# Rows for a token sort: transposed by DMA from the fp16 halves instead of by fp32 transposes on TensorE

## The reference

```python
xp = x @ Wx + b
h_t = tanh(xp_t + h_{t-1} @ Wh)               # 1024 steps, 2 sequences
shared = silu(h @ shared_w1.T) @ shared_w2.T   # 256 -> 1024 -> 256
logits = h @ gate_w.T                          # 8 experts
gates, idx = top_k(logits, 2); gates = softmax(gates)
selected = sum over the two chosen e of gate_e * (silu(h @ experts_w1[e].T) @ experts_w2[e].T)
out = x + shared + selected
```

## Time and profile before

| | us |
|---|---|
| median of 3 runs | 385.0 (383.47 to 388.58) |
| the profiled execution, its own time | 381.38 |
| its span in the trace | 379.7 |
| PE busy | 356.2 (94%) |
| DVE busy | 200.2 (53%) |
| ACT busy | 244.1 (64%) |
| POOL busy | 108.5 (29%) |
| granted TensorE clock, mean | 0.991 of full speed |

### The profile page before, as it was taken

The page is one execution under the profiler, slowest core; times in us unless marked ns, Lnnn a source line. Parts: engine busy times, 40 slices in busy tenths (PEclk is TensorE's granted clock), DMA queues, the critical chain, the costliest instruction groups (busy, mean ns, idle before and its releaser), DMA issues.

```text
span 379.7 us, 8904 instructions
## 1 busy us (share of the span) xinstructions
PE 356.2 (94%) x2458; PEld 253.0 (67%) x2459; DVE 200.2 (53%) x415; ACT 244.1 (64%) x478; POOL 108.5 (29%) x99
## 2 busy tenths in 40 slices
PE   5989999997997998999999999999999999999981
PEld 4758889964664675666667666667766666666660
DVE  0089999979996988964333323333323333232310
ACT  3777788888556778865555665556665556665530
POOL 1100010000276788600123333223333133332241
PEclk9999999999999999999999999999999999999996
DMA  6999999607697979999898998889988989989992
GB/s 194 422 421 434 428 407 334 194 4 124 87 199 182 225 180 226 235 194 196 176 129 153 168 155 155 147 149 156 158 149 154 148 142 158 148 159 147 152 127 28
DMA packets 158173, 73.50 MB, mean 194 GB/s; under 512 B 140736, under 2 KB 155200, under 8 KB 156992
## 3 DMA queue, kind: packets, MB, share of 16 engines
q1 hardware_dynamic: 146672, 59.83, 66.9%
q0 software_dynamic: 6864, 9.11, 16.9%
q10 hardware_dynamic: 4608, 4.20, 4.1%
HBM read 23.68 MB, written 16.53 MB: 106 GB/s over the span
## 4 chain that ended last, share of the span: by engine, by line
PE 80%; ACT 6%; DMA 5%; issue 3%; DVE 2%; another core or an unknown queue 1%; ACTq 1%; POOL 0%; SPq 0%; DVEq 0%; POOLq 0%
PE py L1138 32%; PE z L1033 30%; PE z L1047 8%; PE z L982 3%; PE z L1014 3%; DMA space<-recurrence_w 2%; DMA space<-space 2%; ACT space L799 1%; ACT space L876 1%; PE px L1025 1%; PE py L982 1%; PE z L995 1%; DMA space<-x_cols 1%; ACTq L896 1%
## 5 line engine op out<-in xcount | busy, mean ns | idle before, releaser
L1138 PE MATMUL py<-w_slots,space 128*128 (+1 forms) x1272 | 148.4, 273 | 7.4 <-DMA space<-recurrence_w 3.7
L1033 PE MATMUL z<-w_slots,x 128*128 (+1 forms) x636 | 145.9, 379 | 0.8 <-issue 0.8
L1138 PEld LDWEIGHTS py<-w_slots,space 128*128 128x128 f16 x1272 | 123.8, 98 | 33.1 <-issue 3.5
L1033 PEld LDWEIGHTS z<-w_slots,x 128*128 128x128 f16 x636 | 62.1, 98 | 65.0 <-issue 1.2
L453 POOL DMA_INDIRECT out<-space x37 | 57.5, 1553 | 157.0 <-issue 65.2
L876 ACT ACTIVATE space<-z,tile_scales 128x512 f32<-128x512 f32 x106 | 71.8, 678 | 41.3 <-PE z L1033 34.1
L582 DVE SCALAR_TENSOR_TENSOR recurrence_w<-space,tile_scales,recurrence_w 128x512 f16<-128x512 f32 x54 | 40.5, 750 | 71.7 <-ACT recurrence_w L881 65.6
L582 DVE SCALAR_TENSOR_TENSOR space<-space,tile_scales 128x512 f16<-128x512 f32 x52 | 39.0, 750 | 57.7 <-ACT space L881 42.4
L528 DVE SCALAR_TENSOR_TENSOR w_slots<-w_slots,w_scale 128x1024 f16<-128x1024 f32 x36 | 46.2, 1283 | 1.3 <-issue 0.3
L881 ACT ACTIVATE recurrence_w<-space,tile_scales 128x512 f16<-128x512 f32 x54 | 39.0, 722 | 8.7 <-ACT space L876 2.5
L430 POOL DMA_INDIRECT sorted_rows<-space x32 | 39.1, 1221 | 17.5 <-issue 13.1
(11 more groups left out here) (114 smaller groups left out, 178.9 us busy)
## 6 DMA issues: line engine op xcount, KB each, us to landing
w_slots<-weights SPq DMA_DIRECT2D x9, 2048.0 KB, 30.5
sorted_rows<-pad_row SPq DMA_DIRECT2D x1, 5070.0 KB, 60.2
space<-x_rows ACTq DMA_DIRECT2D x16, 128.0 KB
out<-space ACTq DMA_DIRECT2D x16, 128.0 KB
space<-x_cols SPq DMA_DIRECT2D x1, 1024.0 KB, 8.6
space<-recurrence_w SPq DMA_TRANSPOSE x54
space<-space SPq DMA_TRANSPOSE x52
x<-sorted_rows SPq DMA_TRANSPOSE x39
```

What stands on the lines that cost most here:

```text
L1033: last = nc.tensor.matmul(Z[u % 2][h][:], x16[:, u, x_part, k], weight(f, k * HID + h * BANK, BANK, part), start=k == 0 and x_part == 0 an ...
L1138: last = nc.tensor.matmul(PY[p][:, 0:D], hiddenT[:, p, low, q], weight(f, MATRIX + q * D, D, part), start=q == 0 and not low and part == 0 ...
```

## The change

The three functions that turned the rows on PE, ACT and DVE (`rows`, `sort_row`, `row_low`) are gone, and with them the PSUM bank PX1 and three semaphores. SP gets `turn_row`: one transposing DMA for each tile, from `x16[:, t % RING]` (128 x 512 fp16) into the row of `hr`. `ROWS_AT` says behind which `turn(g)` it is issued: tiles 0, 1 and 2 behind `turn(0)`, tile 3 behind `turn(1)`, none behind `turn(2)`, 4 and 5 behind `turn(3)`, 6 and 7 behind `turn(4)`, and tile g + 3 behind `turn(g)` from g = 5 on. It waits for `x_lo_ok`, for `routed` at tile 4 (and so for all behind it), and for `sorted_ok` from tile 8 on.

The states' halves are made three tiles ahead (`STATES_AT`): tiles 2 and 3 at g = 0, tile g + 3 at g. Before ACT writes tile t >= 4 to the ring of four, it waits for `row_in[t % RING]`, the landing of the row DMA of tile t - 4. POOL's scatters wait for `row_in` in place of `row_ok`. A row of `hr` is 4 fp32 numbers longer (`ROW_PITCH`).

```diff
@@ -52,6 +52,7 @@
...
 ROW = D + META
+ROW_PITCH = ROW + 4
 SORT_RING = 8
...
@@ -87,8 +88,8 @@
...
 AHEAD = 2
-SORT_FROM = 2
-SORT_TILES = TILES // 2
+ROWS_AT = {0: (0, 1, 2), 1: (3,), 3: (4, 5), 4: (6, 7), **{t - 3: (t,) for t in range(8, TILES)}}
+STATES_AT = {0: (2, 3), **{t - 3: (t,) for t in range(4, TILES)}}
 EARLY_WIDES = 6 * WIDES - 2
...
@@ -171,10 +172,10 @@
...
 
-        hr = carve(SORT_RING, ROW)
+        hr = carve(SORT_RING, ROW_PITCH)
         hr16 = hr.rearrange("p u r -> p (u r)").bitcast(F16).rearrange("p (u r) -> p u r", u=SORT_RING)
         after_rows = at[0]
-        at[0] = RING * ROW
+        at[0] = RING * ROW_PITCH
         onehot = carve(TOP, TILES, E)
...
@@ -229,8 +230,7 @@
...
         ahead = [Z[0], Z[1], PY]
-        PX, PX1 = (ctx.enter_context(nc.psum_tensor(f"px{u}", [P, BANK], F32)) for u in range(2))
-        row_bank = [PX, PX1]
+        PX = ctx.enter_context(nc.psum_tensor("px", [P, BANK], F32))
 
...
@@ -264,7 +264,8 @@
...
         turned = [[sem(f"turned_{part}{p}") for p in range(2)] for part in ("hi", "lo")]
-        row_mm, row_hi, row_ok, row_copied = sem("row_mm"), sem("row_hi"), sem("row_ok"), sem("row_copied")
+        row_in = [sem(f"row_in{u}") for u in range(RING)]
+        row_copied = sem("row_copied")
         sorted_ok = [sem(f"sorted_ok{u}") for u in range(SORT_RING)]
...
@@ -343,8 +344,20 @@
...
 
+            def turn_row(t):
+
+                sp.wait_ge(x_lo_ok, t + 1)
+                if t == RING:
+                    sp.wait_ge(routed, 1)
+                if t >= SORT_RING:
+                    sp.wait_ge(sorted_ok[t % SORT_RING], 16 * TOP)
+                sp.dma_start_transpose(hr16[:, t % SORT_RING, 0:2 * D].rearrange("p (a n) -> p a n", n=P),
+                                       x16[:, t % RING].rearrange("p a k n -> p (a k n)")).then_inc(row_in[t % RING], 16)
+
             for g in range(TILES):
                 turn(g, g % 2)
+                for t in ROWS_AT.get(g, ()):
+                    turn_row(t)
                 if g == TILES - 3:
...
@@ -425,11 +438,11 @@
...
                     pool.wait_ge(row_copied, t - SORT_RING + 1)
-                waited(row_ok, t + 1)
+                waited(row_in[t % RING], 16 * (t // RING + 1))
                 for k in range(TOP):
...
                         out=sorted_slots, out_offset=bass.IndirectOffsetOnAxis(slots_u[:, t, k:k + 1], 0),
-                        in_=hr[:, t % SORT_RING], in_offset=None).then_inc(sorted_ok[t % SORT_RING], 16)
+                        in_=hr[:, t % SORT_RING, 0:ROW], in_offset=None).then_inc(sorted_ok[t % SORT_RING], 16)
                 if RING <= t < TILES - RING:
...
@@ -584,11 +597,6 @@
...
 
-            def row_low(t):
-                dve.wait_ge(row_hi, t + 1)
-                nc.vector.scalar_tensor_tensor(hr16[:, t % SORT_RING, D:2 * D], row_bank[t % 2][:, 0:D], STATE_SCALE,
-                                               hr16[:, t % SORT_RING, 0:D], ALU.mult, ALU.subtract).then_inc(row_ok, 1)
-
             def shared_y(g):
...
@@ -710,7 +718,8 @@
...
             route_gap()
-            states_low(2)
+            for t in STATES_AT[0]:
+                states_low(t)
             for h in range(HALVES):
...
@@ -718,15 +727,9 @@
...
                 hidden_low(g, g % 2, n, 0)
-                row = 2 * (g - 1 - SORT_FROM)
-                sorting = 0 <= row < TILES
-                if g + AHEAD < TILES:
-                    states_low(g + AHEAD)
-                if sorting:
-                    row_low(row)
+                for t in STATES_AT.get(g, ()):
+                    states_low(t)
                 hidden_low(g, g % 2, n, 1)
-                if sorting:
-                    row_low(row + 1)
                 if g == 1:
...
@@ -880,14 +883,6 @@
...
 
-            def sort_row(t):
-                act.wait_ge(row_mm, t + 1)
-                if t == RING:
-                    act.wait_ge(routed, 1)
-                if t >= SORT_RING:
-                    act.wait_ge(sorted_ok[t % SORT_RING], 16 * TOP)
-                nc.scalar.mul(hr16[:, t % SORT_RING, 0:D], row_bank[t % 2][:, 0:D], STATE_SCALE).then_inc(row_hi, 1)
-
             def store(g):
...
@@ -907,26 +902,22 @@
...
             hidden_half(0, 0, None, 0)
-            shared_rows(2, x_hi_ok)
+            for t in STATES_AT[0]:
+                shared_rows(t, x_hi_ok)
             hidden_half(0, 0, None, 1)
...
             for g in range(1, TILES):
-                row = 2 * (g - 1 - SORT_FROM)
-                sorting = 0 <= row < TILES
                 n = 16 * (g // 2) if g >= 2 else None
                 hidden_half(g, g % 2, n, 0)
-                if g + AHEAD < TILES:
-                    shared_rows(g + AHEAD, x_hi_ok)
-                elif g + 1 == TILES:
+                for t in STATES_AT.get(g, ()):
+                    act.wait_ge(row_in[t % RING], 16 * (t // RING))
+                    shared_rows(t, x_hi_ok)
+                if g + 1 == TILES:
                     act.wait_ge(tiles_ok, 1)
-                if sorting:
-                    sort_row(row)
                 hidden_half(g, g % 2, n, 1)
-                if sorting:
-                    sort_row(row + 1)
                 if g <= WIDES // 2:
...
@@ -1140,23 +1131,10 @@
...
 
-            def rows(t):
-
-                if t >= 2:
-                    pe.wait_ge(row_ok, t - 1)
-                for k in range(K):
-                    last = nc.tensor.transpose(row_bank[t % 2][:, k * P:(k + 1) * P], states[:, k, t + 1], identity[:])
-                last.then_inc(row_mm, 1)
-
             def expert(t):
...
             for g in range(TILES):
-                sorting = SORT_FROM <= g < SORT_FROM + SORT_TILES
-                if g == SORT_FROM:
-                    pe.wait_ge(prefix_read, 1)
-                if sorting:
-                    rows(2 * (g - SORT_FROM))
                 if g + AHEAD == TILES:
...
@@ -1164,8 +1142,6 @@
...
                     up(g + AHEAD, (g + AHEAD) % RING, expert(g + AHEAD - TILES), 16)
-                if sorting:
-                    rows(2 * (g - SORT_FROM) + 1)
                 down(g, g % 2, 16 * (g // 2 + 1), SHARED)
...
             def iteration(t, u, n, arrived, up_next=True):

```

## The result

The changed kernel takes 390.7 us (median of 4 runs, 388.1 to 391.8), the kernel before beside it 384.5 (383.5 to 388.6). The ratio is 1.0174 [1.0136, 1.0213]: slower by 1.7%, where 381.5 was forecast, and outside the range of 375.5 to 389.5. The profiled execution of after took 391.55 us with a span of 389.8, against 381.38 and 379.7. So there are 10.1 us to be found between two traces.

What follows compares the result with a forecast made beforehand. PE was taken to bound the kernel, with DVE until about 122 us and the DMA engines from 105 us near their limit. -1.5 - 1.8 - 1.2 + 0.5 + 0.5 = -3.5 us gave 381.5 us (median), range 375.5 to 389.5.

Steps and rivals of the forecast that it cites:

- The start: At g = 1 ACT waits for row 0 and goes on 4.6 us late; `hidden_low(1, 1)` on DVE starts 2.7 us late.
- To `down(5)`: From `hidden_low(1, 1)` to `down(5)`: DVE loses six `row_low` and some idle time, so `down(5)` comes 1.5 us earlier.
- both idle times: DVE's waits of 1.69 and 0.99 us for ACT before `shared_y(3)`, both after ACT's hold of 4.96 us.
- Edits with no cost: Edits priced at nothing: the pitch of the rows, one PSUM bank less, the fewer waits of POOL.
- The upper bound: Worst case for `down(5)`: +1.0 us if ACT's hold comes back elsewhere and the row lands late.
- Rows and late halves: PE from `down(5)` to `down(10)`: -1.8 us for eight rows' transposes gone, -1.2 (0 to -2.4) for turned halves less late.
- DMA engines: Tiles g = 10 to 13: the rows' added packets fill the DMA engines and cost +0.5 us (0 to +6).
- the rival: DMA engines as the bound: at a share of 1.12 a tile takes 5.9 us; 382.4 profiled, 386 median; chance 0.21.
- the slower rival: On SP's ring, tiles 3 to 13, a row costs as much as a whole half: +7.0, 388.4 or 392; chance 0.12.
- the DMAs in series: Each transposing DMA keeps the next one out, so sixteen rows cost 30 us: 411 us; chance 0.01.
- The hand-over: SP waits at g = 13 for all scatters, row 15 coming late, before the first load: +0.5 us (0 to +2).
- The forecast's list: Signs of being wrong: turned halves of 7 us or more, later `row_in` waits, PE standing over 2 us at `down(14)` or `up(16)`.

Runs made afterwards that it cites:

- f1_paced: The changed kernel, with POOL waiting for `up(t + 2)` before the scatters of tiles 4 to 8; 380.7 us, 0.9975 of the kernel before.
- f4_one_pause: The changed kernel, with POOL waiting for `up(6)` before the scatters of tile 4 alone; 381.1 us, 0.9966 of the kernel before.
- f2: The kernel before, with POOL's first scatter waiting until row 5 is ready; 396.6 us, 1.0354 of the kernel before.
- g2: The kernel before, with POOL's scatter of row 2 waiting for the first half of `up(6)`; 387.3 us, 1.0082 of the kernel before.
- g3_pause_early: The changed kernel with rows 0 and 1 issued ahead of `turn(0)` and one POOL pause at tile 4; 379.1 us, 0.9898 of the kernel before.
- g1: As g3_pause_early, and from g = 5 on the row's DMA goes between the two halves of `turn(g)`; 378.0 us, 0.9869 of the kernel before.
- e4: The kernel before with the states' halves made three tiles ahead, rows still turned on PE; 382.3 us, 1.0021 of the kernel before.
- f3: As g1, but with the POOL waits of f1_paced (tiles 4 to 8); 381.7 us, 0.997 of the kernel before.

## Why the prediction was wrong

**The start: right.** Row 0 held ACT for 4.09 us (4.6 forecast), and it went on at 93.45 (93.4 forecast), by the timeline of ACT of the changed kernel:

```profile
93.45 0.42 ACT L828 ACTIVATE x<-states 128x256 f16<-128x256 f32 x1 [4.09 <-DMA space<-x]
```

`hidden_low(1, 1)` started at 95.32, 95.1 forecast. The row itself took about 2.5 us from its issue at 90.9, in the bounds of 1.24 and 3.75 and below the 3.0 taken.

**To `down(5)`: the step that failed.** "After: 95.1 + 29.7 - 2.5 = 122.3 with both idle times, 119.6 with neither", and from this 120.6 was taken and `down(5)` counted at -1.5 us. DVE's part of it held: `shared_y(3)` started at 119.66, close to the end with neither idle time. PE had begun `up(7)` at 117.88 and would have been through at 120.5, so `down(5)` 2.1 us earlier than before, not later. What came was 133.41; without the stand, f1_paced has `down(5)` at 121.29 and f4_one_pause at 121.99. The step took the lists of ACT, DVE and SP for all that PE can wait for, and had POOL down as relieved: under "Edits with no cost" stand "the fewer waits of POOL". These waits were the pauses in POOL's run. With `row_ok` gone, which ACT and DVE had fed at their own pace, 18 scatters follow closely on one another, and after seven to twelve of a run PE starts its matmuls one at a time (nine in the changed kernel). This cost 12.9 us (120.5 to 133.41) and 1.3 for the lower clock behind it. Not all of it comes back with a pause: the trace of f4_one_pause is 11.4 us shorter than the changed kernel's, and the two ratios are 8 us apart. f1, f4 and f2 show cause and remedy: one pause of 1.94 us removes it, and a run made long and close in the kernel before brings it.

**The upper bound missed too.** "+1.0 if the hold comes back elsewhere" allowed for the 4.96 us hold of the earlier trace rows to come again at its old size. It was a row of the trace that no semaphore explained, and I gave it a small price and no mechanism. It is probably of the same kind: ACT stood at 111.28, 8 us into a run of eight scatters, and PE had a gap of 0.72 us ("issue") before 114.76 in the same run. That was not shown; g2, made to test it, shortened it and made others.

**Rows and late halves: right.** Up to `down(10)` the forecast had -1.8 of rows and -1.2 of halves, with -2.4 as the halves' bound. PE ran without a gap, and all of the 4.2 us came back, less 1.3 for the clock. Some of that is luck, as the long stand had let the halves get ahead. Where there was none, PE still waited for halves (0.83 and 0.86 us in f4_one_pause), and the same five tiles took 28.1 us in f4, 27.1 in f1_paced and 27.5 in g3_pause_early, by the timelines, against 30.1 before: -2.0, -3.0 and -2.7, where -3.0 was forecast.

**DMA engines: the rival fell.** From 150 to 164 us, with a row in each tile, PE of the changed kernel was busy 14.00 of 14 us at a DMA share of 1.17, where 1.27 was forecast. +0.5 was counted, 0 is right. With it fall the slower rival, whose rows were to make a tile 6.3 us long, and the DMAs in series: every tile from 137 to 178 us took 5.21.

**The hand-over: right place, too small.** +0.5 was counted. By the chain row 15 landed at 168.68 and POOL began it 1.97 us later; the second scatter then took **5.57** us to land from its issue, where "about 1.5 for their landing" stood, and the load 4.33 more. PE waited 3.14 us at `up(16)`. The forecast's list had named this as what would prove it wrong. The Trainium skill, DMA: Bandwidth & Descriptors, section Anatomy of one DMA, gives some 2.0 us as the fixed part of a DMA issued by GpSimd and warns of writes to HBM. The traces show 5.57 here and 3.21 in g3_pause_early, for scatters of 128 rows, both above it.

With the missing mechanism out of the way, f1_paced and f4_one_pause come out at 0.9975 and 0.9966 of before. The forecast, 381.5 of 385.0, is 0.991: some 2 us of the 3.5 are missing. In f4_one_pause they lie in two places. Ahead of the hand-over, `down(5)` comes 0.6 us earlier than before (1.5 forecast) and the next five tiles gain 2.0 (3.0 forecast), so that it would have reached `up(16)` at 168.48, 2.6 us earlier than before. At the hand-over it then waits 0.42 us, and 1.40 at `down(14)`, where +0.5 was counted; f1_paced waits 1.92 and 0.42. g3 and g1, which start earlier, are at 0.990 and 0.987.

## What to carry to other kernels

A wait on an engine off the critical path can be of use: before it is taken out as free, ask what this engine then does without a pause, and for how long. Long runs of indirect DMAs from POOL, 1.45 us or less apart as here, belong broken up, by a wait on something that the busy engine counts anyway. A look at POOL's idle time alone doesn't find them: the kernel before had 20 scatters without idle time and took no harm. And a hold in the trace before that no semaphore explains is a cost without a known size; price it by what could make it longer, not by its length.

## What the runs showed of the hardware

While POOL issues indirect DMAs closely one behind another (1.36 to 1.45 us from start to start over a run), PE's matmuls start singly after some 8 to 16 us, and 2 to 4 us behind the end of the run PE is at pace again. Runs of 16 to 20 scatters at 1.64 to 1.77 us (before, e4, f3, f4, g3) did not do this. In the changed kernel's stretch the starts of PE's groups of one or two matmuls lie 0.71, 2.45, 1.43, 1.40, 2.12, 2.12, 2.84 and 1.43 us apart, nearly all multiples of 0.71, here three of them:

```profile
122.47 0.58 PE L1024 MATMUL z<-w_slots,x 128*128 128x512 f16 x1 [1.05 <-issue]
123.87 0.59 PE L1024 MATMUL z<-w_slots,x 128*128 128x512 f16 x1 [0.82 <-issue]
125.99 1.30 PE L1024 MATMUL z<-w_slots,x 128*128 128x512 f16 x2 [1.52 <-issue]
```

That looks like instructions that have to be fetched and are fetched late. It is not shown. The DMA queues of the trace have one for instructions, "q8 instruction", and after 108 us its next packet comes only at 136 to 138 us in the changed kernel, when PE has long resumed, and at 132 to 134 us in f4_one_pause, where PE never stopped. Of a second one, "q14 instruction", two packets fall into the 15 us in either kernel. The rows of q8, changed kernel and f4_one_pause:

```profile
q8 instruction: 1, 0.02, 3.5%
```
```profile
q8 instruction: 1, 0.02, 2.9%
```

So a late packet of these queues doesn't explain it. Which resource POOL's issuing takes from PE stays open, and so do the spacing from which on it happens and how short a pause is enough.

Two transposing DMAs of different size cost SP the same: a row of 128 x 512 is issued in 1.24 us, as a half of 128 x 1024 is the earlier trace rows:

```profile
L354 SPq DMA_TRANSPOSE space<-x x16: 1202/1244/1747, 90.9 to 166.7; - x16
```
